# Second MLP product from fp16 halves, its halves made on GpSimd, norms of the input and the output partly moved to ScalarE and GpSimd

## The chip, the cores and the metric

One NeuronCore of one Trainium2 chip runs the whole program. The engines are TensorE (PE, its weight loads are PEld), VectorE (DVE), ScalarE (ACT), GpSimd (POOL) and the queue of SyncE (SP) that issues every DMA. The metric is the time of one execution in microseconds on the device. A profile of one execution, in which every instruction has a start and a duration, stands beside the times.

## What is computed

The reference, cut to what matters here (`LN` is a layer norm without gain):

```python
x = x + LN(attn(LN(x)))                      # 4 x 2048 x 256, dense attention: first part of the program
h0 = LN(x)
for l in range(2):                           # second part, window by window of 128 rows
    h = shift_token(h0)                      # half of the columns from the row before
    q, k, v = split(h @ wqkv[l])             # 3 x 512 columns, 8 heads of 64
    q, k = rotary(l2norm(q) * qs), rotary(l2norm(k) * ksc)
    o = local_attention(q, k, v)             # a window of 128 sees itself and the one before
    h0 = h0 + o @ wo[l]
    h = LN(shift_token(h0)) * lg + lb
    a, g = split(h @ w1[l] + b1[l])          # 2 x 682 columns
    h0 = h0 + (a * gelu(g)) @ w2[l] + b2[l]  # the second MLP product
x = x + LN(h0)
```

All in float32. The kernel keeps that precision by splitting an operand into a high and a low half and adding three products (high x high, high x low, low x high).

## The kernel before, in words

Rows are handled in windows of 128 rows: 64 windows in each of two layers, so 128 window steps (`NT`). The program has three stages: `phase_a` (dense attention, to 650 us), the preparation of the weights at the head of `phase_b` (650 to 717 us), and the main loop (717 us to the end), which is a software pipeline written out by hand. Each engine runs the same list of slots `s`; `run(s, r, pairs, layer)` holds, engine by engine, the code of one slot, and `slots` (L483) calls it with `r = s % 4`. In slot `s` window `s` has its q, k and v products, window `s-1` its scores, window `s-2` its probabilities times v and its output projection, window `s-3` the normalisation of its MLP input. The MLP itself goes in pairs of windows: in an **even slot** TensorE ends with the first MLP product (L944), in an **odd slot** with the second (L955). Both take inputs from VectorE, which multiplies a and gelu(g) into `hid` at the end of an even slot (L1174).

Nothing is scheduled automatically. The order on an engine is the order in which `run` is written, and an instruction that waits holds everything behind it on its engine or queue; the waits are semaphores. The order on TensorE in a slot: transposes of q and k of the window before (L847, L854), q, k, v products (L869), transposes of the probabilities (L885), probabilities times v (L897), scores (L910), output projection (L923), transpose of the next input (L836), then one of the two MLP products.

Lines that the prediction uses:

- ScalarE: squares of q and k (L981, L983), copies of the transposed probabilities to SBUF, four for a slot (L992), the cast of the attention's output (L995), the exponentials (L1002), gelu (L1015).
- VectorE: rotary terms (L1041 to L1043), statistics of the MLP input (L1107, L1109, L1111), its normalisation (L1117) and high half (L1120), the masked maximum of the scores (L1138), division by the row sum (L1151), `xp` (L1162, the stream after the attention), `xpp` (L1063, the stream after the MLP).
- GpSimd: the power -1/2 of the variance (L1200), the sum of squares by six halvings (L1190), the low half of the MLP input (L1205), sums of the rotary terms (L1209 for q, L1212 for k), the power of 16 sums of squares (L1223), k times its norm (L1228), `xb` (L1234).
- SyncE's queue, in the order of a slot: loads of the next input and tables, the DMA transpose of the halves of the MLP input of window `s-3` (L813), the store of `xp` of window `s-2` (L819), and its shifted load back as `h2` (L823, L824). The transpose waits for both halves:

```python
sp.wait: xh_hi, xh_lo of t = s-3  ->  dma_start_transpose(h2T, xh_hl)      # L813
sp.wait: xp_ready of t = s-2      ->  dma_start(xp_v, xp) -> load h2       # L819, L823, L824
```

## Time and profile before

| | value |
|---|---|
| median of 3 runs (lowest, highest) | 3122.34 us (3121.93, 3125.83) |
| the profiled execution | 3122.74 us, its span 3120.9 us |
| TensorE's granted clock, mean | 0.979 of full speed |
| PE busy | 2969.0 us, 95% |
| PEld busy | 2577.5 us, 83% |
| DVE busy | 2654.2 us, 85% |
| ACT busy | 1876.3 us, 60% |
| POOL busy | 1742.8 us, 56% |

The shares are means over the three stages and say little by themselves; the main loop is 77% of the span. A pair of slots (one even, one odd) takes 36.55 us in it, and 64 pairs make it up. "Busy" of TensorE counts overlapping matmuls once, and the time that one matmul adds is the distance between starts, not its duration.

### The profile page before, as it was taken

Reading aid. Unit: us, or ns where it says so; the run is one execution under the profiler, and the core shown is the slowest. Engines: PE = TensorE matmul, PEld = TensorE weight load, DVE = VectorE, ACT = ScalarE, POOL = GpSimd, SP = SyncE. Lnnn points to the kernel's source line nnn. Section 1 sums busy time; section 2 is a strip of 40 time slices with the busy share of each in tenths; the row PEclk is TensorE's granted clock in tenths of the full one; section 3 lists DMA queues with packets and bytes.
Section 4 is the critical chain, followed back from the end, with each engine's and each line's share of the span. In section 5 each row is a group of like instructions: output and inputs, shape, how many; then the busy total and the mean of one; then the engine's idle time right before and its main releaser. Section 6 shows DMA issues by size and latency. Waiting matters only on the chain.

```text
span 3120.9 us, 79791 instructions
## 1 busy us (share of the span) xinstructions
PE 2969.0 (95%) x24952; PEld 2577.5 (83%) x24952; DVE 2654.2 (85%) x7701; ACT 1876.3 (60%) x4322; POOL 1742.8 (56%) x2070
## 2 busy tenths in 40 slices
PE   7999999945999999999999999999999999999997
PEld 4868686844888888888888888888888888888886
DVE  7889898656888888888888888898999999999995
ACT  6252525113666666667666766666666667666763
POOL 0313131125666666666666666676776677767763
PEclk9999999967999999999999999999999999999998
DMA  1212121151111111111111111122221211122121
GB/s 39 62 48 64 46 63 40 54 202 53 47 50 49 56 47 50 52 49 47 50 54 50 49 54 48 51 57 61 61 56 58 59 55 55 58 64 59 56 58 43
DMA packets 273326, 177.65 MB, mean 57 GB/s; under 512 B 95758, under 2 KB 271090, under 8 KB 272754
## 3 DMA queue, kind: packets, MB, share of 16 engines
q1 hardware_dynamic: 273138, 175.50, 19.2%
q8 instruction: 74, 1.21, 0.2%
q14 instruction: 114, 0.93, 0.1%
HBM read 104.08 MB, written 54.54 MB: 51 GB/s over the span
## 4 chain that ended last, share of the span: by engine, by line
PE 73%; POOL 1%; issue 1%; DVE 1%; ACT 0%; DMA 0%; POOLq 0%; SPq 0%; DVEq 0%; ACTq 0%
PE b_ps L869 17%; PE b_ps L944 14%; PE b_ps L955 10%; PE b_ps L897 8%; PE b_ps L885 7%; PE b_ps L923 6%; PE b_ps L910 6%; PE b_ps L854 2%; PE b_ps L847 2%; PE b_ps L836 1%; POOL b_sq L1190 0%; POOL b_rn L1223 0%; DVE b_probs L1138 0%; POOL b_t L1212 0%; DVE b_probs L1151 0%
## 5 line engine op out<-in xcount | busy, mean ns | idle before, releaser
L1002 ACT ACTIVATE b_probs<-b_probs,b_negmax 128x256 f32<-128x256 f32 x1024 | 505.9, 495 | 78.4 <-DVE b_negmax L1138 77.5
L869 PE MATMUL b_ps<-b_wqkv,b_hT_hi 128*128 128x512 f32 x1536 | 492.0, 402 | 1.0 <-DVE b_hT_lo L1026 1.0
L944 PE MATMUL b_ps<-b_h2T,b_w 128*128 128x256 f16 x4224 | 474.4, 274 | 6.4 <-DMA b_h2T<-b_xh_hl 6.4
L944 PEld LDWEIGHTS b_ps<-b_h2T,b_w 128*128 128x128 f16 x4224 | 414.5, 98 | 55.3 <-DMA b_h2T<-b_xh_hl 6.8
L1190 POOL TENSOR_TENSOR b_sq<-b_sq 128x512 f32<-128x512 f32 (+5 forms) x768 | 418.5, 545 | 60.6 <-ACT b_sq L983 20.3
L1223 POOL TENSOR_TENSOR b_rn<-b_ss_min,b_mhalf 128x16 f32<-128x16 f32 x128 | 377.5, 2949 | 109.2 <-DVE b_ss_min L1050 109.0
L1151 DVE TENSOR_SCALAR b_probs<-b_probs,b_rinv 128x256 f32<-128x256 f32 x1024 | 409.6, 442 | 18.2
L1200 POOL TENSOR_TENSOR b_rstd<-b_var,b_mhalf 128x1 f32<-128x1 f32 x128 | 72.0, 562 | 552.9 <-DVE b_var L1111 552.9
L452 PE MATMUL a_ps<-a_xn_hl,a_E 128*128 128x256 f16 x3072 | 344.5, 273 | 8.8 <-DVE a_E L318 8.8
L955 PE MATMUL b_ps<-b_w,b_hid 128*128 128x256 f32 x1536 | 342.2, 379 | 1.2 <-DVE b_hid L1174 1.2
L452 PEld LDWEIGHTS a_ps<-a_xn_hl,a_E 128*128 128x128 f16 x3072 | 299.4, 98 | 44.2 <-ACT a_e L397 9.6
L869 PEld LDWEIGHTS b_ps<-b_wqkv,b_hT_hi 128*128 128x128 f32 x1536 | 282.7, 191 | 54.3 <-ACT b_hT_hi L967 1.4
L1138 DVE CUSTOM_DVE_ANT_0 b_probs<-b_ps,b_mask,b_rn 128x256 f32<-128x256 f32 x768 | 324.5, 478 | 0.0
L955 PEld LDWEIGHTS b_ps<-b_w,b_hid 128*128 128x128 f32 x1536 | 286.8, 190 | 37.9 <-DVE b_hid L1174 1.5
L869 PE MATMUL b_ps<-b_wqkv,b_hT_lo 128*128 128x512 f32 x768 | 302.7, 394 | 0.0
L992 ACT COPY b_probsT<-b_ps 128x512 f32<-128x512 f32 x512 | 264.0, 611 | 4.5 <-PE b_ps L885 4.2
L1015 ACT ACTIVATE b_gl<-b_ps,b_b,b_w_unit 128x256 f32<-128x256 f32 (+1 forms) x384 | 202.8, 561 | 102.8 <-DVE b_hid L1174 70.4
L897 PE MATMUL b_ps<-b_probsT,b_v 128*64 128x128 f32 x4096 | 252.3, 276 | 0.0
L885 PE MATMUL b_ps<-b_ident_f,b_probs 128*128 128x128 f32 x2048 | 245.5, 273 | 3.5 <-DVE b_xpp L1063 2.3
L885 PEld LDWEIGHTS b_ps<-b_ident_f,b_probs 128*128 128x128 f32 x2048 | 232.2, 141 | 20.0 <-DVE b_xpp L1063 2.5
L897 PEld LDWEIGHTS b_ps<-b_probsT,b_v 128*64 128x64 f32 x4096 | 221.4, 137 | 21.6 <-ACT b_probsT L992 18.1
L1174 DVE SCALAR_TENSOR_TENSOR b_hid<-b_ps,b_b1a,b_gl 128x256 f32<-128x256 f32 (+1 forms) x384 | 177.0, 478 | 53.3 <-ACT b_gl L1015 46.9
(139 smaller groups left out, 6218.8 us busy)
## 6 DMA issues: line engine op xcount, KB each, us to landing
b_hx<-xs_dram SPq DMA_DIRECT2D x256, 64.0 KB, 1.9
b_rot<-rot_dram SPq DMA_DIRECT2D x128, 128.0 KB, 2.1
b_xr<-xs_dram SPq DMA_DIRECT2D x128, 128.0 KB, 2.0
xp_dram<-b_xp SPq DMA_DIRECT2D x128, 128.0 KB, 1.8
b_h<-xp_dram SPq DMA_DIRECT2D x256, 64.0 KB, 1.8
a_x_res<-in_L_attn_x_dram SPq DMA_DIRECT2D x64, 128.0 KB, 2.2
x_dram<-a_x SPq DMA_DIRECT2D x64, 128.0 KB, 1.7
xs_dram<-a_xo SPq DMA_DIRECT2D x64, 128.0 KB, 1.8
```

Of the source, the lines that this page charges most:

```text
L452: last = nc.tensor.matmul(ps[:, bank, 0:D], E[:, j, a, i * P:(i + 1) * P], xn_hl[:, b % 2, j, c, :], start=(j == 0 and a == 0 and c == 0), ...
L869: last = nc.tensor.matmul(ps[:, bank, :], hT[:, k, :], wqkv[:, ds(layer(s), 1), part, k, bank * INNER:(bank + 1) * INNER], start=(k == 0 a ...
L885: last = nc.tensor.transpose(ps[:, 3 + p, n * P:(n + 1) * P], probs[:, 2 * p + n // 2, (n % 2) * P:(n % 2 + 1) * P], ident_f[:])
L897: last = nc.tensor.matmul(ps[h * DH:(h + 1) * DH, 7, p * P:(p + 1) * P], v[:, window, (2 * p + h) * DH:(2 * p + h + 1) * DH], probsT[:, p, ...
L944: last = nc.tensor.matmul(ps[:, bank, half * 2 * P:(half + 1) * 2 * P], w1[:, ds(layer(2 * j), 1), wp, k, first:first + P], h2T[:, hp, k, ...
L955: last = nc.tensor.matmul(ps[:, 3, n * D:(n + 1) * D], hid[:, c, n * P:(n + 1) * P], w2[:, ds(layer(2 * j), 1), c, :], start=(c == 0), sto ...
L992: nc.scalar.copy(probsT[:, p, :], ps[:, 3 + p, :]).then_inc(pT_kept, 1)
L1002: nc.scalar.activation(probs[:, h, :], probs[:, h, :], ACT.Exp, bias=negmax[:, h:h + 1], scale=-1.0, accum_out=rowsum[:, h:h + 1]).then_in ...
L1138: nc.vector.tensor_tensor_reduce(probs[:, h, :], head_scores(h), which, rn[:, (r - 1) % 2, h:h + 1], ABOVE_ALL, ALU.add, ALU.min, negmax[: ...
L1151: nc.vector.tensor_scalar(probs[:, h, :], probs[:, h, :], rinv[:, h:h + 1], None, ALU.mult).then_inc(probs_ready, 1)
L1190: nc.gpsimd.tensor_tensor(target, target, sq[:, :, width:2 * width], ALU.add).then_inc(ss_halved, 1)
L1223: nc.gpsimd.tensor_tensor(rn[:, r % 2, :], ss_min[:], mhalf[:], ALU.pow).then_inc(rn_ready, 1)
```

## The change

1. **Second MLP product.** `hid` and `w2` are split into fp16 halves, and the 12 float32 matmuls of a pair of windows become 36 fp16 ones. `w2` is scaled and split while the weights are prepared, which also takes new bounds (maxima of `w2` and the bias, a second reduction over partitions). The halves of `hid` are made by GpSimd: a cast and a subtraction for each of six blocks, four blocks at the end of the even slot, two in the odd slot.
2. **MLP input.** Statistics (`norm_stats`) stand ahead of `xpp` on VectorE; the addition of epsilon and a new term `shift2` go to GpSimd; the normalisation and the high half go to ScalarE as two ACTIVATE Identity, in the even slot ahead of the four copies of the probabilities, in the odd slot behind the cast of the attention's output. The low half (GpSimd) stays early in the even slot; in the odd slot it now stands behind `hid`'s halves and behind k's norm.
3. **Norms of q and k.** One halving on GpSimd and one VectorE reduction in place of six halvings; the power is taken in two parts of 8 columns, k's first.
4. **Output of layer 2.** Statistics and their power in the even slot, the normalisation itself on ScalarE in the odd slot.
5. **VectorE.** Two rotary instructions where three were, two reciprocals where four were, `xp` ahead of the divisions.
6. **ScalarE.** The copy of v stands behind the copies of the probabilities.

The diff, cut (semaphore names, allocations and renamed counts are left out):

```diff
@@ preparation of the weights
+                for l in range(LAYERS):
+                    nc.scalar.activation(w2[:, l, 0], w2_f[:, l], ACT.Copy, scale=w2_scale[:, l:l + 1]).then_inc(w2_hi, 1)
...
-                        pool.wait_ge(top_ready, LAYERS)
+                        pool.wait_ge(top_ready, 4 * LAYERS)
+                        nc.gpsimd.partition_all_reduce(top_all..., top..., P, RED_MAX).then_inc(top_shared, 1)
+                        nc.gpsimd.partition_all_reduce(sq_all[:], top_sq[:], P, RED_ADD).then_inc(top_shared, 1)
...
+                    nc.vector.scalar_tensor_tensor(w2[:, l, 1], w2_f[:, l], w2_scale[:, l:l + 1], w2[:, l, 0], ALU.mult, ALU.subtract)
@@ TensorE, odd slot
-                        pe.wait_ge(hid_ready, HC * (j + 1))
+                        pe.wait_ge(hid_lo, HC * (j + 1))
                         for n in range(2):
                             for c in range(HC):
-                                last = nc.tensor.matmul(ps[:, 3, n * D:(n + 1) * D], hid[:, c, n * P:(n + 1) * P], w2[:, ds(layer(2 * j), 1), c, :],
-                                                        start=(c == 0), stop=(c == HC - 1))
+                                for a, (hp, wp) in enumerate(PARTS):
+                                    last = nc.tensor.matmul(ps[:, 3, n * D:(n + 1) * D], hid_hl[:, hp, c, n * P:(n + 1) * P],
+                                                            w2[:, ds(layer(2 * j), 1), wp, c, :], ...)
@@ ScalarE
+                def normalise_input(t, r):
+                    if in_range(t):
+                        act.wait_ge(shift2_ready, t + 1)
+                        wait(act, xh_lo, t)
+                        nc.scalar.activation(xh[:], h2[:, (r - 3) % 2, :], ACT.Identity, bias=shift2[:], scale=rstd2[:]).then_inc(xh_ready, 1)
+                        wait(act, h2T_loaded, 16 * t)
+                        nc.scalar.activation(xh_hl[:, 0, :], h2[:, (r - 3) % 2, :], ACT.Identity, bias=shift2[:], scale=rstd2[:]).then_inc(xh_hi, 1)
...
                         nc.scalar.activation(sq[:, HEADS:2 * HEADS, :], by_head(ps[:, 1, :]), ACT.Square).then_inc(k_sq, 1)
+                    if r % 2 == 0:
+                        normalise_input(s - 3, r)
...
+                            nc.scalar.copy(probsT[:, p, :], ps[:, 3 + p, :]).then_inc(pT_kept, 1)
...
                         nc.scalar.copy(oT[:, 0], by_pair(ps[:, 7, :])).then_inc(oT_hi, 1)
+                    if r % 2 == 1:
+                        normalise_input(s - 3, r)
@@ VectorE
+                    norm_stats(s, r)
                     layer_output(pairs - 3, r, layer)
-                    (statistics of the MLP input)
                     rotate(s, r, 0, q_sq, q_terms, qr_ready)
-                        nc.vector.tensor_scalar(xh[:], h2[:, (r - 3) % 2, :], mv2[:, 0:1], rstd2[:], ALU.subtract, ALU.mult).then_inc(xh_ready, 1)
-                        nc.vector.tensor_copy(xh_hl[:, 0, :], xh[:]).then_inc(xh_hi, 1)
                     rotate(s, r, 1, k_sq, k_terms, kr_ready)
                     output_stats(pairs - 3, r, layer)
+                    sum_squares(s)
@@ GpSimd
+                        nc.gpsimd.tensor_scalar(var2[:], mv2[:, 1:2], EPS, None, ALU.add).then_inc(var2_ready, 1)
                         nc.gpsimd.tensor_tensor(rstd2[:], var2[:], mhalf[:, 0:1], ALU.pow).then_inc(rstd2_ready, 1)
+                        nc.gpsimd.tensor_scalar(shift2[:], mv2[:, 0:1], rstd2[:], -1.0, ALU.mult, ALU.mult).then_inc(shift2_ready, 1)
+                    if r % 2 == 1:
+                        hid_halves(pairs - 2, HID_EARLY, HC)     # cast and subtraction, blocks 4 and 5
+                    if r % 2 == 0:
+                        input_low(s - 3)
...
+                    if r % 2 == 1:
+                        input_low(s - 3)                         # behind kr
...
+                    if r % 2 == 0:
+                        hid_halves(pairs - 2, 0, HID_EARLY)      # blocks 0 to 3
```

The order on GpSimd in an odd slot of the main loop, in the kernel before, from the power of the variance to `xb`:

```order
L1200 TENSOR_TENSOR b_rstd2<-b_var2,b_mhalf 128x1 [waits b_var2_ready]
L1190 TENSOR_TENSOR b_sq<-b_sq 128x16x32 [waits b_ss_halved]
L1190 TENSOR_TENSOR b_sq<-b_sq 128x16x16 [waits b_ss_halved]
L1205 TENSOR_TENSOR b_xh_hl<-b_xh,b_xh_hl 128x256 [waits b_h2T_loaded]
L1209 TENSOR_TENSOR b_qr<-b_t1,b_t2 128x512 [waits b_qT_done,b_q_terms]
L1190 TENSOR_TENSOR b_sq<-b_sq 128x16x8 [waits b_ss_halved]
...
L1212 TENSOR_TENSOR b_t1<-b_t1,b_t2 128x512 [waits b_k_terms]
L1223 TENSOR_TENSOR b_rn<-b_ss_min,b_mhalf 128x16 [waits b_scores_kept]
L1228 TENSOR_TENSOR b_kr<-b_t1,b_rn 128x512 [waits b_kT_done,b_kr_sum,b_rn_ready]
L1234 TENSOR_TENSOR b_xb<-b_xp,b_b2 128x256 [waits b_xpp_ready]
```

The same place in the changed kernel (`b_hid_hl` are the halves of `hid`, `b_xh_hl` those of the MLP input, `b_rn_k` is k's norm):

```order
L1265 TENSOR_SCALAR b_var2<-b_mv2 128x1 [waits b_mv2_ready]
L1268 TENSOR_TENSOR b_rstd2<-b_var2,b_mhalf 128x1 [waits b_xh_hi,b_var2_ready]
L1270 TENSOR_SCALAR b_shift2<-b_mv2,b_rstd2 128x1 [waits b_rstd2_ready]
L1274 TENSOR_TENSOR b_sq<-b_sq 128x16x32 [waits b_k_sq]
L1246 CAST b_hid_hl<-b_hid 128x256 [waits b_hid_ready]
L1248 TENSOR_TENSOR b_hid_hl<-b_hid,b_hid_hl 128x256 [waits b_hid_hi]
...
L1282 TENSOR_TENSOR b_qr<-b_t1,b_t2 128x512 [waits b_qT_done,b_q_terms]
L1284 TENSOR_TENSOR b_t1<-b_t1,b_t2 128x512 [waits b_k_terms]
L1288 TENSOR_SCALAR b_ss_min<-b_ss 128x16 [waits b_ss_summed]
L1290 TENSOR_TENSOR b_rn_k<-b_ss_min,b_mhalf 128x8 [waits b_ss_ready]
L1294 TENSOR_TENSOR b_kr<-b_t1,b_rn_k 128x512 [waits b_kT_done,b_kr_sum,b_rnk_ready]
L1255 TENSOR_TENSOR b_xh_hl<-b_xh,b_xh_hl 128x256 [waits b_h2T_loaded]
```

The low half of the MLP input was the fourth instruction of the slot and is now behind k's product, with the two blocks of `hid` ahead of it as well.

The order on ScalarE in an even slot of the kernel before, from the cast of k to the cast of the attention's output:

```order
L977 CAST b_kT<-b_ps 128x4x128 [waits b_kT_done]
L981 ACTIVATE b_sq<-b_ps 128x512 [waits b_q_done,b_ss_ready]
L983 ACTIVATE b_sq<-b_ps 128x512 [waits b_k_done]
L986 COPY b_v<-b_ps 128x512 [waits b_pv_done,b_v_done]
...
L992 COPY b_probsT<-b_ps 128x512 [waits b_pT_done]
...
L995 CAST b_oT<-b_ps 128x512 [waits b_wo_done,b_pv_done]
```

And in the changed kernel:

```order
L1046 CAST b_kT<-b_ps 128x4x128 [waits b_kT_done]
L1051 ACTIVATE b_sq<-b_ps 128x512 [waits b_q_done,b_ss_summed]
L1055 ACTIVATE b_sq<-b_ps 128x512 [waits b_k_done]
L1034 ACTIVATE b_xh<-b_h2,b_shift2,b_rstd2 128x256 [waits b_xh_lo,b_shift2_ready]
...
L1036 ACTIVATE b_xh_hl<-b_h2,b_shift2,b_rstd2 128x256 [waits b_h2T_loaded]
...
L1063 COPY b_probsT<-b_ps 128x512 [waits b_pT_done]
...
L1067 COPY b_v<-b_ps 128x512 [waits b_pv_done,b_v_done]
L1072 CAST b_oT<-b_ps 128x512 [waits b_wo_done,b_pv_done]
```

Two instructions that wait for `shift2` now stand ahead of the four copies of the probabilities, and v's copy has moved behind them.

## Rows read from the trace of the kernel before

**Rows 1.** Busy time by stretch: stretch, length, then each engine, granted clock, DMA share.
```profile
900.00:1900.00 1000.00, 1000.00 (x8599) 892.51 (x8598) 863.77 (x2679) 686.75 (x1695) 641.00 (x728) 1.00 0.18 51
```

**Rows 2.** Timeline of PE, an odd and an even slot: start, duration, instruction.
```profile
1503.95 0.60 PE L847 MATMUL b_ps<-b_ident_f,b_qr 128*128 128x128 f32 x4
...
1516.05 5.34 PE L955 MATMUL b_ps<-b_w,b_hid 128*128 128x256 f32 x24
1521.23 0.60 PE L847 MATMUL b_ps<-b_ident_f,b_qr 128*128 128x128 f32 x4
...
1528.05 1.97 PE L897 MATMUL b_ps<-b_probsT,b_v 128*64 128x128 f32 x32
...
1533.30 7.37 PE L944 MATMUL b_ps<-b_h2T,b_w 128*128 128x256 f16 x66
1540.50 0.60 PE L847 MATMUL b_ps<-b_ident_f,b_qr 128*128 128x128 f32 x4
```

**Rows 3.** Groups of POOL by form: count, busy us, mean ns, idle before.
```profile
L1223 POOL TENSOR_TENSOR b_rn<-b_ss_min,b_mhalf 128x16 f32<-128x16 f32 x128 | 377.5, 2949 | 109.2 <-DVE b_ss_min L1050 109.0
L1212 POOL TENSOR_TENSOR b_t<-b_t 128x512 f32<-128x512 f32 x128 | 165.5, 1293 | 0.0
L1228 POOL TENSOR_TENSOR b_kr<-b_t,b_rn 128x512 f32<-128x512 f32 x128 | 133.4, 1042 | 10.0
L1205 POOL TENSOR_TENSOR b_xh_hl<-b_xh,b_xh_hl 128x256 f16<-128x256 f32 x128 | 86.4, 675 | 40.0 <-DVE b_xh_hl L1120 40.0
L1200 POOL TENSOR_TENSOR b_rstd<-b_var,b_mhalf 128x1 f32<-128x1 f32 x128 | 72.0, 562 | 552.9 <-DVE b_var L1111 552.9
L1190 POOL TENSOR_TENSOR b_sq<-b_sq 128x16 f32<-128x16 f32 x128 | 28.3, 221 | 10.0
L1196 POOL COPY b_mask_now<-b_mask 128x256 bf16 x27 | 11.6, 429 | 0.0
```

**Rows 4.** Timeline of ACT: the odd slot's squares of k, the even slot's copies.
```profile
1507.79 0.60 ACT L983 ACTIVATE b_sq<-b_ps 128x512 f32<-128x512 f32 x1 [0.72 <-PE b_ps L869]
...
1526.96 2.06 ACT L992 COPY b_probsT<-b_ps 128x512 f32<-128x512 f32 x4
```

**Rows 5.** Timeline of SyncE's queue, the odd slot's transpose, store and last load.
```profile
1512.10 1.22 SPq L813 DMA_TRANSPOSE b_h2T<-b_xh_hl  x1
1519.25 0.36 SPq L819 DMA_DIRECT2D xp_dram<-b_xp  x1
...
1521.65 0.38 SPq L824 DMA_DIRECT2D b_h<-xp_dram  x1
```

**Rows 6.** Timeline early in the loop, from a store of xp to the statistics.
```profile
787.79 0.35 SPq L819 DMA_DIRECT2D xp_dram<-b_xp  x1
...
791.82 0.42 DVE L1107 BATCH_NORM_STATS2 b_st<-b_h 128x6 f32<-128x256 f32 x1
792.38 0.18 DVE L1109 BATCH_NORM_AGGREGATE b_mv<-b_st 128x2 f32<-128x6 f32 x1
```

**Rows 7.** Groups of ACT by form: the exponentials and gelu.
```profile
L1002 ACT ACTIVATE b_probs<-b_probs,b_negmax 128x256 f32<-128x256 f32 x1024 | 505.9, 495 | 78.4 <-DVE b_negmax L1138 77.5
L1015 ACT ACTIVATE b_gl<-b_ps,b_b,b_w_unit 128x256 f32<-128x256 f32 x320 | 166.8, 561 | 101.0 <-DVE b_hid L1174 70.4 <-PE b_ps L944 28.9
```

**Rows 8.** Waits from 900 to 3100 us: total, times, longest.
```profile
PEld b_ps L897 <- ACT b_probsT L992: 17.7, 106, 0.2
```

**Rows 9.** Timeline of the preparation of the weights: low halves of w1.
```profile
697.56 9.15 POOL L613 TENSOR_TENSOR p_rot_all<-p_rot_all,p_head_scale 128x4096 f32<-128x4096 f32 x1 [6.92 <-issue]
697.96 11.71 DVE L672 SCALAR_TENSOR_TENSOR b_w<-p_w_f,p_w_scale,b_w 128x2816 f16<-128x2816 f32 x1
...
710.73 3.14 DVE L672 SCALAR_TENSOR_TENSOR b_w<-p_w_f,p_w_scale,b_w 128x2816 f16<-128x2816 f32 x1
```

**Rows 10.** Timeline of PE in the second slot of the loop.
```profile
737.11 1.12 PE L854 MATMUL b_ps<-b_ident_f,b_kr 128*128 128x128 f32 x4 [5.72 <-POOL b_kr L1228]
```

**Rows 11.** Group of DVE by form: the maximum over a layer's w1.
```profile
L654 DVE TENSOR_REDUCE p_top<-p_w_f 128x1 f32<-128x2816 f32 x2 | 6.2, 3086 | 0.1
```

More of the change, by code:

```diff
@@ new lines, in _ @@
+                    dve.wait_ge(top_ready, l + 1)
+                    nc.vector.tensor_tensor(top_sq[:, l:l + 1], top[:, 0, l:l + 1], top[:, 0, l:l + 1], ALU.mult)
+                dve.wait_ge(loaded_mlp, 16 * DMAS_MLP)
+                dve.wait_ge(cleared, 4)
+                for l in range(LAYERS):
+                    nc.vector.tensor_tensor(b1[:, l, :], ps[:, l, 0:W1_BLOCKS], b1_f[:, l, :], ALU.add).then_inc(bias_added, 1)
+                    nc.vector.tensor_reduce(top[:, 2, l:l + 1], w2_f[:, l].rearrange("p c d -> p (c d)"), AX.X, ALU.max, apply_absolute_value=True).then_inc(top_ready, 1)
@@ new lines, in _ @@
+                for l in range(LAYERS):
+                    dve.wait_ge(bias_added, l + 1)
+                    nc.vector.tensor_reduce(top[:, 1, l:l + 1], b1[:, l, :], AX.X, ALU.max, apply_absolute_value=True).then_inc(top_ready, 1)
+                    nc.vector.tensor_scalar(top_sq[:, l:l + 1], top_sq[:, l:l + 1], 2.0, None, ALU.mult).then_inc(top_ready, 1)
+                dve.wait_ge(top_shared, 2)
+                nc.vector.tensor_tensor(bias_sq[:], top_all[:, 1, :], top_all[:, 1, :], ALU.mult).then_inc(step, 1)
@@ L1166, in run @@
                     normalise(3)
-                    output_norm(pairs - 3, r, layer)
                     j = pairs - 2
                     if r % 2 == 0 and in_range(2 * j):
-                        wait(dve, w2_done, j)
+                        wait(dve, hid_lo, HC * j)
                         for c, bank in enumerate(W1_BANKS):
@@ L1234, in run @@
                         nc.gpsimd.tensor_tensor(xb[:, (r - 2) % 4, :], xp[:, r % 2, :], b2[:, ds(layer(t), 1), :], ALU.add).then_inc(xb_ready, 1)
+                    j = pairs - 3
+                    f = j - NW // 2
+                    if r % 2 == 0 and in_range(2 * j) and layer(2 * j) == 1:
+                        wait_apart(pool, mvf_ready, 2 * f + 2, passed_pool)
+                        nc.gpsimd.tensor_scalar(varf[:], mvf[:, :, 1], EPS, None, ALU.add).then_inc(varf_ready, 1)
+                        pool.wait_ge(varf_ready, f + 1)
+                        wait(pool, xf_ready, 2 * f)
+                        nc.gpsimd.tensor_tensor(rstdf[:], varf[:], mhalf[:, 0:2], ALU.pow).then_inc(rstdf_ready, 1)
+                        wait_apart(pool, rstdf_ready, f + 1, passed_pool)
+                        for n in range(2):
+                            last = nc.gpsimd.tensor_scalar(shiftf[:, n:n + 1], mvf[:, n, 0:1], rstdf[:, n:n + 1], -1.0, ALU.mult, ALU.mult)
+                        last.then_inc(shiftf_ready, 1)
+                    if r % 2 == 0:
+                        hid_halves(pairs - 2, 0, HID_EARLY)
                     j = pairs - 3
```

288 lines of the change are left out of this document (159 added, 129 removed).

## The prediction

> **What bounds the kernel now.** I read the busy times by stretch first. In a stretch of 1000 us in the main loop TensorE is busy for all of it, at full clock, VectorE for 864 us and GpSimd for 641 us [rows 1]. The loop is bound by TensorE, so work taken from it is gained unless another chain takes over. Then TensorE's timeline, to get the length of each slot and the distances: the odd slot goes from 1503.95 to 1521.23 (17.28 us), the even one to 1540.50 (19.27 us), 36.55 us a pair; the second product takes 1521.23 - 1516.05 = 5.18 us of the odd one, the first product 1540.50 - 1533.30 = 7.20 us for 66 fp16 matmuls [rows 2]. Then the other engines' timelines, to see how much later each thing that TensorE waits for may come. The closest is in the list of waits: the weight loads of "probabilities times v" (L897) waited for ScalarE's copy 106 times, 0.17 us each [rows 8], so that copy arrives with little to spare in nearly every slot.
>
> **The second product.** 66 matmuls in 7.20 us is 0.109 us for one of fp16 with 256 columns. 36 of them are 3.93 us, where 24 halves of float32 matmuls took 5.18 [rows 2]. TensorE is relieved of 1.25 us a pair, 80 us over 64 pairs, and the odd slot becomes 16.03 us.
>
> **What the moved steps do to the queue.** I follow one pair, with 0 at the start of its odd slot. The squares of k end at 1507.79 + 0.60, which is 4.44 [rows 4]; the power of the variance is over at about the same time. GpSimd then has, in order: one halving of 512 columns; cast and subtraction of two blocks of `hid`; the sums for q and k; a floor of 16 columns; a power of 8; k times its norm; and only then the low half of the MLP input. The sums are 1.29 each, the halving the same size (1.29), subtraction and low half 0.67, k's product 1.04, the floor 0.22 [rows 3]. The power took 0.56 for 1 column and 2.95 for 16, 0.159 a column, so 1.68 for 8 [rows 3]. The cast isn't in the trace: from below a bf16 copy of 256 columns, 0.43, less what a float32 source might save (nothing that I can show, so I allow 0.2), from above the subtraction's 0.67, as it reads less [rows 3]; I take 0.43, the nearest row. With 0.07 for each of four waits on a result just made: 4.5 + 1.29 + 2 x (0.43 + 0.07 + 0.67) + 2 x 1.29 + 0.22 + 0.07 + 1.68 + 0.07 + 1.04 + 0.67 = 14.4. Before, the transpose that waits for it went out 7.15 us ahead of the store of `xp` [rows 5], so its place cost nothing.
>
> Now it does. SyncE's queue waits for this low half before the transpose, and behind the transpose stand the store of `xp` and its load back. Transpose 0.3 after the low half, 1.22 of issue, 0.2 to the next: the store goes out at 16.15, though `xp` is made earlier than before, when the store went at 1519.25, which is 15.30 [rows 2, 5]. From a store's issue to the statistics of the loaded rows it was 791.82 - 787.79 = 4.03 us where VectorE was waiting for them [rows 6]; in the main loop the last load is issued 2.40 after the store [rows 5], 0.2 more. So `h2` is there at 20.35, which is 4.3 after the start of the even slot (at 16.03).
>
> **What then waits.** In the even slot VectorE, which is past the low halves of q and k at about 2.6, waits for `h2` until 4.3. From statistics to mean and variance 0.74 [rows 6]: 5.1. On GpSimd: epsilon 0.2, power 0.56, shift 0.2 [rows 3], and 0.35 of waits: 6.4. ScalarE has no such ACTIVATE in its rows; by exponentials (0.50) and gelu (0.56) with 0.1 overlap, two of 256 columns take 0.9 to 1.0, from below 0.8 (two exponentials, each 0.1 overlapped), from above 1.1 (two of gelu's) [rows 7]. The first copy of the probabilities starts at 7.4. It started at 1526.96, which is 5.73 after the slot's start [rows 2, 4]. How late may it start? It lasts 0.6, and probabilities times v starts at 6.82 [rows 2], with 0.17 of slack already used by waiting weight loads [rows 8]; later copies follow at 0.49 and the products at 0.47, so nothing is caught up. I take 6.05 as the limit. TensorE then stands for 7.4 - 6.05 = 1.35 us in every even slot, and I add 0.15 for GpSimd being held once by VectorE's divisions, which fall into the same stretch: 1.5 us. Against the 1.25 us saved, a pair becomes 0.25 us longer.
>
> That last 0.15 rests on a pair of rows: the same VectorE instruction took 11.71 us beside a GpSimd multiplication of 9.15, and 3.14 without it [rows 9]. The Trainium skill ("SBUF — State Buffer", Who interferes with whom) has this as an exclusive lock of a port that the two engines share, held for a whole instruction by whoever starts first. By that rule, the trace agrees (9.15 + 3.14 is 12.3, less the part where they did not overlap), and one more collision would be worth 0.3 us at most.
>
> The Trainium skill ("GPSIMD Engine Reference", 3.1 Elementwise) puts one-input work at about 1.03 cycles an element and two-input work at 2.6. By the first the cast would be about 0.22 us plus its start, an estimate from that page, and the sum would fall by 0.1 to 0.2 us a pair; no row here has a float32 cast on GpSimd, so the sum goes by the rows above.
>
> **The other edits.** VectorE loses the normalisation and the high half, two of four reciprocals and some rotary overhead and gains one reduction; it was not the bound [rows 1], and its gain is idle time. ScalarE's two ACTIVATE in the odd slot stand ahead of the exponentials and push them by 0.9; the low half of the next input then comes within 0.1 of its need in the even slot, and up to 0.7 late if a GpSimd addition is in the way. That stall would lie in front of the same wait for the copies and so be a part of the 1.5, not on top of it. `hid`'s halves are ready by 8.0 of the odd slot, TensorE wants them at 12.1: nothing. The first product's input in the even slot still has some 2 us to spare. The output's norm moves to where ScalarE idles between the squares; GpSimd has at most 1.5 us more of it per pair, behind which stand `hid`'s first four blocks, and those have room: nothing.
>
> **Outside the steady loop.** Preparation: VectorE's chain runs from the maxima (3.09 for 2816 columns, so 1.7 for the 1536 of `w2`, twice [rows 11]) through some fifteen tiny steps instead of five (+2), then the low halves of `w2` (3.14 x 1536/2816, 1.7 twice [rows 9]) and its share of a wait on the second reduction (+1). 3.4 + 2 + 3.4 + 1 and 0.7 for small pieces: 10.5 us, from 4 (if part of it lies under loads) to 16. Filling of the pipeline: TensorE waited 5.72 us for k's norm [rows 10], and the slot behind it about as long; in this chain one halving replaces six (-2.0), a power of 8 one of 16 (-1.3), so 3.1 less twice, and `xp` ahead of the divisions gives about 1.2 twice: -8.5, from -12 to -4. End: the last halves of `hid` stand alone (+1.1, cast and subtraction), and two more hand-overs: +2.5, less or more by 2.
>
> **Sum.** The stall falls in 61 pairs. 3122.74 (the profiled execution: its span of 3120.9 and 1.8 around it) - 80 + 61 x 1.5 + 10.5 - 8.5 + 2.5 = 3138.7. The profiled execution is 0.4 above the median of the runs shown, so I forecast 3138 us.
>
> **Range of this case.** The chain is long, and each 0.1 us in it is 6 us of time. With the low ends (cast 0.23, no waits, two ACTIVATE at 0.8, the copy's limit 0.3 later) the stall is near 0.5: 3078. With the high ends (cast 0.67, power of 8 at 2.0, waits 0.15, two collisions) near 2.4: 3193.
>
> **Rivals.**
>
> *A: the chain has slack, TensorE stays the bound.* The low half of the MLP input comes soon enough, or the store isn't held by it. For it: the chain crosses two slots, and `xp` itself is made earlier, ahead of four divisions. Against it: the queue is in order, and the start of the copies leaves 0.3 us. With no stall: 3122.74 - 80 + 4.5 = 3047. With a stall of 0.5 it passes into the low end above. It decides once the stall is under 1.24 us (61 x 1.24 is the 80 saved less the 4.5 added outside the loop). This is the faster side.
>
> *B: GpSimd becomes the bound.* Per pair it had 23.4 us of work (0.641 of 36.55 [rows 1]). Out go 4.0 of halvings, in come 6.6 for the halves of `hid`, 0.6 to 1.2 for the powers and 1.2 for small ones: 28 to 29 us, in layer 2 some 31.5, of the 35.3 a pair would have. Against it: there remain 4 us, and what it waits for is early. For it: ten instructions more per pair than before, most in chains of two, and waits between them that a sum of durations doesn't hold. At 0.4 us more for each it would be full, and with its fixed places late everywhere: a stall of some 3 us a pair, 3122.74 - 80 + 61 x 3 + 4.5 = 3230. This is the rule of the other side too: the Trainium skill ("GPSIMD Engine Reference", 4.1 Engine selection) would keep elementwise work of two inputs on VectorE, being about twice slower on GpSimd.
>
> *C: nothing to be seen.* Stall and saving cancel within 0.1 us a pair, a point inside the forecast's range: 3117 to 3128.
>
> **Chances.** Forecast with a stall from 1.0 to 2.4: 0.55. A (under 1.0): 0.33, of which no stall at all 0.13. B: 0.12. C lies in the forecast's case with 0.12. 0.2% is 6.2 us, about what a measurement of this kernel can tell from no change. Faster 0.35, the same 0.12, slower 0.53. The range leaves out the clean gain and most of B: 3065 to 3190.
>
> **What would show it.** TensorE's odd slots 16.0 us long in the timeline, with the second product at 3.9; even slots 20.8 instead of 19.3, with TensorE idle ahead of probabilities times v, released by ScalarE's copies. ScalarE waiting for `shift2` in even slots, VectorE's statistics waiting there for the load of `h2` until 4.3 after the slot's start, SyncE's queue waiting for GpSimd's low half in odd slots and storing `xp` about 2.4 us after it is made. The low half at 14.4. The loop begins 10 us later. I am wrong if statistics in even slots wait for nothing, if the low half is done before 13 in the odd slot, or if TensorE waits somewhere else, for k or for `hid`.

## The result and the profile after

The changed kernel took 3188.1 us (median of 4 runs, 3183.9 to 3190.1), the kernel before 3122.1 us beside it: a ratio of 1.0207, 95% interval 1.019 to 1.0225. Slower was forecast, and 3188 lies within the range, but only 16 us of loss were forecast and 66 came.

The busy times of the stretch that [rows 1] shows of before:

```profile
900.00:1900.00 1000.00, 964.07 (x8697) 840.34 (x8696) 772.28 (x2255) 726.37 (x1769) 740.64 (x970) 1.00 0.17 49
```

TensorE, busy for all of the stretch before, now stands for 36 us of it at the same full clock. GpSimd rose from 641 to 741 us, which is 27.8 of the 37.48 us of a pair, far from full: rival B is out. The timeline of PE, an odd slot and the even slot behind it, against [rows 2]:

```profile
1526.42 0.60 PE L898 MATMUL b_ps<-b_ident_f,b_qr 128*128 128x128 f32 x4
...
1538.57 4.09 PE L1007 MATMUL b_ps<-b_w,b_hid_hl 128*128 128x256 f16 x36
1542.50 0.60 PE L898 MATMUL b_ps<-b_ident_f,b_qr 128*128 128x128 f32 x4
...
1544.54 0.73 PE L920 MATMUL b_ps<-b_wqkv,b_hT_hi 128*128 128x512 f32 x2 [1.00 <-DVE b_hT_lo L1105]
...
1549.15 1.96 PE L936 MATMUL b_ps<-b_ident_f,b_probs 128*128 128x128 f32 x16
1551.30 2.11 PE L948 MATMUL b_ps<-b_probsT,b_v 128*64 128x128 f32 x32 [0.19 <-ACT b_probsT L1063]
...
1556.69 7.37 PE L995 MATMUL b_ps<-b_h2T,b_w 128*128 128x256 f16 x66
1563.90 0.49 PE L898 MATMUL b_ps<-b_ident_f,b_qr 128*128 128x128 f32 x3
```

The odd slot is 16.08 us long (17.28 before), the even one 21.40 (19.27): the whole gain of the fp16 product, 1.20 us, is there, and 2.13 us are lost behind it. The pair is 37.48 instead of 36.55. Probabilities times v (L948) starts 8.80 us after the slot's start, 6.82 before. The idle time in front of it carries three names in the list of waits from 900 to 3000 us (total, times, longest):

```profile
DVE b_st L1133 <- DMA b_h<-xp_dram: 66.1, 56, 3.3
PE b_ps L920 <- DVE b_hT_lo L1105: 41.3, 52, 1.0
PEld b_ps L948 <- ACT b_probsT L1063: 27.4, 104, 0.4
PE b_ps L936 <- DVE b_xpp L1149: 24.9, 43, 2.1
```

The first row is the forecast wait of VectorE for the load of `h2`. The third is the copies. The second and fourth, for the low half of the next QKV input and for `xpp`, were not in the sum. The idle times are smaller than the stall, because a stop also ends the overlap of two matmuls: q, k and v start 1.25 us later in their slot than before (2.04 us after its start against 0.79), and the row shows 1.00 of it as idle.

The forecast chain, in the same two slots: GpSimd and SyncE's queue at the end of the odd slot, then VectorE, GpSimd and ScalarE in the even one (against [rows 4, 5]).

```profile
1540.41 0.67 POOL L1255 TENSOR_TENSOR b_xh_hl<-b_xh,b_xh_hl 128x256 f16<-128x256 f32 x1
1541.40 1.22 SPq L864 DMA_TRANSPOSE b_h2T<-b_xh_hl  x1
1542.74 0.50 SPq L870 DMA_DIRECT2D xp_dram<-b_xp  x1
...
1545.27 0.38 SPq L875 DMA_DIRECT2D b_h<-xp_dram  x1
...
1547.26 0.43 DVE L1133 BATCH_NORM_STATS2 b_st<-b_h 128x6 f32<-128x256 f32 x1 [1.24 <-DMA b_h<-xp_dram]
...
1548.14 0.88 DVE L1149 SCALAR_TENSOR_TENSOR b_xpp<-b_ps,b_w_unit,b_xb 128x256 f32<-128x256 f32 x2
...
1549.31 0.26 POOL L1270 TENSOR_SCALAR b_shift<-b_mv,b_rstd 128x1 f32<-128x1 f32 x1 [0.21 <-POOL b_rstd L1268]
...
1549.68 0.60 ACT L1034 ACTIVATE b_xh<-b_h,b_shift,b_rstd 128x256 f32<-128x256 f32 x1 [1.45 <-POOL b_shift L1270]
1550.19 0.59 ACT L1036 ACTIVATE b_xh_hl<-b_h,b_shift,b_rstd 128x256 f16<-128x256 f32 x1
1550.68 2.02 ACT L1063 COPY b_probsT<-b_ps 128x512 f32<-128x512 f32 x4
```

Read it against the slot's start at 1542.50: store at 0.24, statistics at 4.76, shift done at 7.07, first copy at 8.18. `xpp` stands behind the statistics on VectorE, so the same load holds it too.

The distance from one first MLP product to the next, taken over the loop, says how much of the 67.4 us of span (3188.3 - 3120.9) lies where. Before, the median was 36.56 us; after, 37.47, and a few pairs at the loop's start, at the turn of the layers and at the end took 38.2 to 39.4. From the first such product (806.31, before 802.08) to the last (3162.60, before 3096.41) the loop lost 62.0 us; 4.2 were lost ahead of it and 1.2 behind.

### The profile page after: what moved, and what is told of

It reads as the page before. It is cut to its first block and busy times, and to the rows that moved or that the text cites. A ratio compares the mean times of both kernels' runs of the same rounds, so it can differ in the third digit from the quotient of the medians.

```text
span 3188.3 us, 81609 instructions
## 1 busy us (share of the span) xinstructions
PE 2936.1 (92%) x25720; PEld 2504.8 (79%) x25720; DVE 2481.0 (78%) x6734; ACT 2039.5 (64%) x4644; POOL 2063.0 (65%) x2807
## 5 line engine op out<-in xcount | busy, mean ns | idle before, releaser
L920 PE MATMUL b_ps<-b_wqkv,b_hT_hi 128*128 128x512 f32 x1536 | 500.9, 408 | 52.2 <-DVE b_hT_lo L1105 43.7
L1197 DVE CUSTOM_DVE_ANT_0 b_probs<-b_ps,b_mask,b_rn 128x256 f32<-128x256 f32 x768 | 317.6, 478 | 0.0
L1166 DVE TENSOR_TENSOR b_oT<-b_ps,b_oT 128x512 fp32r<-128x512 f32 x128 | 88.5, 691 | 279.0 <-ACT b_oT L1072 279.0
L1248 POOL TENSOR_TENSOR b_hid_hl<-b_hid,b_hid_hl 128x256 f16<-128x256 f32 (+1 forms) x384 | 258.2, 672 | 31.0
L948 PE MATMUL b_ps<-b_probsT,b_v 128*64 128x128 f32 x4096 | 260.3, 280 | 9.9 <-ACT b_probsT L1063 5.9
L1007 PE MATMUL b_ps<-b_w,b_hid_hl 128*128 128x256 f16 x2304 | 261.9, 273 | 3.0 <-POOL b_hid_hl L1248 3.0
L948 PEld LDWEIGHTS b_ps<-b_probsT,b_v 128*64 128x64 f32 x4096 | 217.6, 137 | 47.5 <-ACT b_probsT L1063 28.5
L1007 PEld LDWEIGHTS b_ps<-b_w,b_hid_hl 128*128 128x128 f16 x2304 | 224.7, 98 | 29.0 <-POOL b_hid_hl L1248 3.2
L1265 POOL TENSOR_SCALAR b_var<-b_mv 128x1 f32<-128x1 f32 x128 | 29.8, 233 | 312.2 <-DVE b_mv L1136 312.2
```

Of the source, the lines that this page charges most:

```text
L920: last = nc.tensor.matmul(ps[:, bank, :], hT[:, k, :], wqkv[:, ds(layer(s), 1), part, k, bank * INNER:(bank + 1) * INNER], start=(k == 0 a ...
L948: last = nc.tensor.matmul(ps[h * DH:(h + 1) * DH, 7, p * P:(p + 1) * P], v[:, window, (2 * p + h) * DH:(2 * p + h + 1) * DH], probsT[:, p, ...
L1007: last = nc.tensor.matmul(ps[:, 3, n * D:(n + 1) * D], hid_hl[:, hp, c, n * P:(n + 1) * P], w2[:, ds(layer(2 * j), 1), wp, c, :], start=(c ...
L1197: nc.vector.tensor_tensor_reduce(probs[:, h, :], head_scores(h), which, rn[:, (r - 1) % 2, h:h + 1], ABOVE_ALL, ALU.add, ALU.min, negmax[: ...
L1248: nc.gpsimd.tensor_tensor(hid_hl[rows, 1, c, :], hid[rows, c, :], hid_hl[rows, 0, c, :], ALU.subtract).then_inc(hid_lo, 1)
```

## The experiments

Each ratio is against the kernel before, run beside it on the same chip; its medians there were 3121.9 to 3124.1 us. "Pair" is the median distance from one first MLP product to the next, in layer 1 and layer 2. The first row is the kernel before as it ran beside the changed one.

| kernel | us | ratio (95%) | pair 1, 2 |
|---|---|---|---|
| before | 3122.1 | 1 | 36.56, 36.56 |
| changed | 3188.1 | 1.0207 (1.019-1.0225) | 37.47, 37.46 |
| e1_act_behind | 3240.6 | 1.037 (1.0353-1.0388) | 38.03, 38.46 |
| e2_xpp_first | 3193.1 | 1.0222 (1.0205-1.0239) | 37.43, 37.41 |
| e3_both | 3127.2 | 1.0011 (1.0002-1.0021) | 36.28, 36.52 |
| e4_two_products | 3194.3 | 1.0225 (1.0208-1.0242) | 37.50, 37.49 |
| b1_low_late | 3301.4 | 1.0574 (1.0557-1.0592) | 39.10, 39.72 |
| e5_low_earlier | 3124.5 | 1.0006 (0.9997-1.0016) | 36.46, 36.47 |
| e6_low_keep | 3109.5 | 0.9955 (0.9938-0.9971) | 35.83, 36.74 |
| e7_keep_only | 3188.2 | 1.0209 (1.0192-1.0226) | 37.44, 37.47 |
| e8_all | 3077.2 | 0.9856 (0.984-0.9873) | 35.75, 35.67 |
| e9_store_first | 3131.6 | 1.0029 (1.0018-1.0041) | 36.56, 36.45 |
| e10_low_keep_xpp | 3155.1 | 1.0102 (1.0085-1.0119) | 36.57, 37.50 |
| e11_all_store | 3091.7 | 0.9903 (0.9887-0.992) | 35.77, 36.13 |

**Is it TensorE's work at all? (e4)** One of the three products that make the second MLP product is left out (high halves by low halves), a third of its matmuls.

```diff
-for a, (hp, wp) in enumerate(PARTS):
+for a, (hp, wp) in ((0, (0, 0)), (2, (0, 1))):
```

> Changed kernel with a third of the second MLP product left out (the product of hid's low half and w2's high half, 12 of 36 matmuls); the rest unchanged. It leaves out part of the computation. TensorE is relieved of 12 x 0.109 = 1.31 us in each odd slot, at its end. Theory (a chain that begins at k's squares in the odd slot and runs over GpSimd, SyncE's queue, the store and load of xp, statistics and normalisation to probabilities times v in the next even slot sets the pair): the work stands beside this chain, the even slot's stall grows by what the odd slot loses, 3188 us, within 6. Rival (TensorE is the bound and a fixed stall is added to it): 3188 - 64 x 1.31 = 3104 us.

It took 3194.3 us, 6 above the changed kernel and at the edge of what was expected (the granted clock was a little lower too, 0.971 against 0.978): taking out a third of these matmuls gained nothing. The timeline of PE shows an odd slot shorter by 1.31 us and an even slot longer by 1.18:

```profile
1528.23 0.60 PE L898 MATMUL b_ps<-b_ident_f,b_qr 128*128 128x128 f32 x4
...
1543.00 0.60 PE L898 MATMUL b_ps<-b_ident_f,b_qr 128*128 128x128 f32 x4
...
1565.58 0.60 PE L898 MATMUL b_ps<-b_ident_f,b_qr 128*128 128x128 f32 x4
```

14.77 and 22.58 us, against 16.08 and 21.40 (the median even slot of layer 1 is 22.74). With the stall, what TensorE saves in the odd slot it waits out in the even one: its time is no longer the pair's time.

**Which link holds TensorE? (e2, e1, e3)** e2 puts `xpp` ahead of the output's statistics on VectorE, e1 puts ScalarE's even normalisation behind the copies of the probabilities, e3 does both.

```diff
-norm_stats(s, r)
 layer_output(pairs - 3, r, layer)
+norm_stats(s, r)
```
```diff
-if r % 2 == 0:
-    normalise_input(s - 3, r)
 (copies of the probabilities, L1063)
+if r % 2 == 0:
+    normalise_input(s - 3, r)
```

> Changed kernel, but on VectorE xpp (L1149) stands ahead of the statistics of the MLP input, as it did before the change. Theory (two chains): the transposes of the probabilities start 0.9 us earlier in even slots, but the copies still stand behind the normalisation, so that probabilities times v starts as late: 3188 us, within 5. Rival (xpp behind the late statistics is the cause): 1.2 us a pair gone, 3115 us.

> Changed kernel, but in even slots ScalarE's two normalising ACTIVATE stand behind the four copies of the probabilities, ahead of v's copy. Theory (two chains from the late load of h2 end at TensorE nearly together: one by the normalisation on ScalarE to the copies, one by xpp on VectorE, since the transposes of the probabilities in even slots wait for xpp): only the first is cut, the second still holds the transposes until 6.8 after the slot's start; TensorE's even slot shortens by the 0.2 to 0.3 us between the two, 3188 - 61 x 0.25 = 3173 us. Rival (the normalisation ahead of the copies is the cause, as predicted): the whole stall beyond what k's and q's products wait for goes, 1.2 us a pair, 3115 us.

> Changed kernel with both edits: xpp ahead of the statistics, and the normalisation behind the copies in even slots. Theory (two chains): h2 still lands as late (4.8 after the even slot's start), but nothing that TensorE needs soon hangs on it; left is the stall in front of the q, k, v products, 0.85 us in even slots, for which the low half of the next input comes late (the odd slot's normalisation pushes the exponentials). Even slot 20.1 us, pair 36.2: 3188 - 61 x 1.3 = 3109 us. Rival (the stall is a matter of GpSimd being full, so that it moves elsewhere): 3170 to 3190 us.

e2 held, 5 us above the changed kernel: the wait for `xpp` vanished from the list of waits, and the copies' waits grew by more (in the changed kernel 27.4 us for PEld and 4.4 us in 17 times for PE):

```profile
PEld b_ps L948 <- ACT b_probsT L1063: 59.8, 104, 1.3
PE b_ps L948 <- ACT b_probsT L1063: 41.4, 56, 1.1
```

e1 missed both theories: 3240.6, where a gain had been expected. Its rows, PE, SyncE's queue, VectorE and GpSimd in the even slot that starts at 1517.42, and last two groups of VectorE's divisions later in that slot:

```profile
1518.39 0.51 SPq L870 DMA_DIRECT2D xp_dram<-b_xp  x1
...
1522.84 0.43 DVE L1133 BATCH_NORM_STATS2 b_st<-b_h 128x6 f32<-128x256 f32 x1 [2.24 <-DMA b_h<-xp_dram]
...
1524.72 1.96 PE L936 MATMUL b_ps<-b_ident_f,b_probs 128*128 128x128 f32 x16 [1.49 <-DVE b_xpp L1149]
...
1528.67 0.68 POOL L1255 TENSOR_TENSOR b_xh_hl<-b_xh,b_xh_hl 128x256 f16<-128x256 f32 x1 [2.27 <-ACT b_xh_hl L1036]
...
1533.82 1.93 DVE L1209 TENSOR_SCALAR b_probs<-b_probs,b_rinv 128x256 f32<-128x256 f32 x4
...
1536.74 1.09 DVE L1209 TENSOR_SCALAR b_probs<-b_probs,b_rinv 128x256 f32<-128x256 f32 x2
```

TensorE no longer waits for the copies but for `xpp`, and the chain has become longer: the store goes out 0.97 us after the slot's start (0.24 in the changed kernel), because GpSimd, held 2.27 us by the later normalisation, is late for the rest of the even slot. The way from there to the store leads over VectorE. A division takes 0.35 us alone. In the changed kernel only GpSimd's `xb` (0.7 us) falls beside the divisions, and one of them takes 0.82; in e1 k's product (1.04 us, from 1534.04) falls beside one of the first four, which takes 1.14, and `xb` (from 1536.69) beside one of the last two, which takes 0.82. The eight of an even slot take 4.03 us instead of 3.26 (medians of layer 1), so the statistics of the next odd slot start 3.18 us into it instead of 2.61, GpSimd waits for them, and the low half, the transpose and the store move with them. That the overlap lengthens the divisions is read from these rows; no run takes it away alone. So each of the two moves alone opens one of two doors behind the same load. With both open (e3) the time fell by 61 us, to 3127.2, 18 above what I expected: q, k and v still wait 24.2 us in all for `hT_lo`, and layer 2 is 0.24 us a pair longer than layer 1. In e3 the load of `h2` is even later than in the changed kernel (statistics 5.43 us into the even slot against 4.77, medians of layer 1); TensorE just doesn't wait for it.

**Is it the late low half? (b1, e5, e9)** b1 makes this one move in the kernel before. e5 moves it back by a power and a product in the changed kernel. e9 leaves GpSimd alone and lets the store pass the transpose on the queue.

```diff
 (b1, in the kernel before; e5 the reverse, to behind kr_sum)
-input_low(s - 3)            # behind halve(s, 0, 2)
+if r % 2 == 1: input_low(s - 3)   # behind the product kr
```
```diff
 (e9, odd slots)
-transpose of xh_hl (s-3); store of xp, loads of h2 (s-2)
+store of xp, loads of h2 (s-2); transpose of xh_hl (s-3)
```

> One part of the change alone: in the kernel before, only the odd slots' second half of the MLP input is moved, from behind the first halvings to behind the key product (before 1511.10 in a slot that begins at 1503.95, then about 1520.2 on GpSimd). Theory (the chain odd GpSimd, transpose, store of the output, load of the next MLP input, statistics, ScalarE is what the move lengthens): the transpose is issued about 1521.1 and the store about 1522.5 against 1519.25 before, so the MLP input lands 3.2 us later in the even slot and the copies of the probabilities start about 3.4 us late; 2 to 3.4 us for each of 61 pairs, 3240 to 3330 us. Rival (the move falls into slack, and the loss of the changed kernel is GpSimd's new work or TensorE's): 3122 +- 6 us.

> The changed kernel with one instruction moved back: the odd slots' second half of the MLP input stands behind the key terms' sum, ahead of the power for the key product (about 11.5 us into the slot instead of 14.1). Theory (the same chain): the store then waits for the output alone, about 13.9 us into the slot against 16.3, so the MLP input lands 2.4 us earlier in the even slot, ScalarE's normalisation ends before TensorE's transposes of the probabilities, and both the wait for the copies (about 1.1 us) and that for the shortcut (0.5 us) go; the wait for the second half of the QKV input (0.85 us) stays. Pair of slots 36.6 to 36.9 us against 37.49: 3133 to 3151 us. Rival (the waits for copies and shortcut come from GpSimd's work on the odd slot as a whole, whatever its order): 3188 +- 6 us.

> The changed kernel with one move on the DMA queue: in odd slots the store of the attention output and the loads of the next MLP input stand ahead of the transpose of the MLP input's halves; GpSimd's order stays as changed, with its odd second half at 14.1 us. Theory (the late second half costs only because the transpose that waits for it stands ahead of the store in the queue): the store goes at about 13.9 us instead of 16.3, and the time is that of the kernel with the second half moved back, 3118 to 3132 us. Rival (the order on GpSimd itself, or the late transpose, costs): 3175 to 3200 us.

b1: +179 us by this move alone, 2.9 us a pair, inside the theory's 3240 to 3330. But the door was another than I had named. There VectorE itself normalises, and the wait for the load holds everything behind it on that engine, the attention's output `oT` at last (SyncE's queue, VectorE, TensorE):

```profile
1533.78 0.51 SPq L819 DMA_DIRECT2D xp_dram<-b_xp  x1
...
1538.36 0.43 DVE L1107 BATCH_NORM_STATS2 b_st<-b_h 128x6 f32<-128x256 f32 x1 [3.38 <-DMA b_h<-xp_dram]
...
1543.35 0.67 DVE L1090 TENSOR_TENSOR b_oT<-b_ps,b_oT 128x512 fp32r<-128x512 f32 x1
...
1544.08 2.63 PE L923 MATMUL b_ps<-b_wo,b_oT 128*128 128x256 f32 x12 [1.94 <-DVE b_oT L1090]
```

Not all of the 179 us is waiting. From 900 to 3100 us TensorE stood 110.4 us in 56 times for `oT`, and its granted clock fell to the lower level behind half of these stops (29 times, 99 us in all, each time within 1.5 us of the first matmul behind one), as in the stretch that begins with the last row (length, busy times, clock):

```profile
1544.00:1547.00 3.00, 2.92 (x15) 2.86 (x16) 3.00 (x15) 2.54 (x11) 2.66 (x6) 0.58 0.22 44
```

The 12 matmuls of that row took 2.63 us where they take 1.68 at full clock. Over the loop the clock was 0.98 (900 to 1900 us) and 0.97 (2000 to 3000 us), against 1.00 in both for the kernel before and the changed one. 99 us at half the clock do the work of 50, so up to some 50 of the 179 us, an estimate, are the price of the lower clock behind the waits and not the waits themselves.

e5: 3124.5 us, 64 less than the changed kernel (I had said 3133 to 3151; the pair is 36.46, a little under my 36.6). The same place, SyncE and PE:

```profile
1516.91 1.22 SPq L864 DMA_TRANSPOSE b_h2T<-b_xh_hl  x1
1518.90 0.36 SPq L870 DMA_DIRECT2D xp_dram<-b_xp  x1
...
1521.14 0.60 PE L898 MATMUL b_ps<-b_ident_f,b_qr 128*128 128x128 f32 x4
...
1522.95 0.72 PE L920 MATMUL b_ps<-b_wqkv,b_hT_hi 128*128 128x512 f32 x2 [0.78 <-DVE b_hT_lo L1105]
...
1527.24 1.91 PE L936 MATMUL b_ps<-b_ident_f,b_probs 128*128 128x128 f32 x16
1529.08 1.97 PE L948 MATMUL b_ps<-b_probsT,b_v 128*64 128x128 f32 x32
```

The store goes 2.24 us ahead of the even slot's start instead of 0.24 behind it, the waits for `xpp` are gone, those for the copies are back near their size of before (19.6 us of weight loads in 106 times, 17.7 before), and one is left, for `hT_lo`. e9 held at 3131.6. Its rows, SyncE's queue and GpSimd in the odd slot from 1510.83 to 1526.91:

```profile
1524.67 0.35 SPq L873 DMA_DIRECT2D xp_dram<-b_xp  x1
1524.82 0.67 POOL L1265 TENSOR_TENSOR b_xh_hl<-b_xh,b_xh_hl 128x256 f16<-128x256 f32 x1
...
1527.82 1.22 SPq L865 DMA_TRANSPOSE b_h2T<-b_xh_hl  x1
```

The low half starts 13.99 us into the slot, as late as in the changed kernel, but the store goes 2.24 us ahead of the even slot, as in e5, and 57 of the 66 us of loss are gone. So it is the order on the queue, the store behind a transpose that waits for GpSimd, that carries the delay; that is shown from both sides.

**The wait under the wait (e7, e6)** Both make `hT_lo` ahead of the second group of divisions on VectorE, e7 in the changed kernel, e6 in e5.

```diff
-normalise(2)
 if in_range(s + 1):
     keep_hT(s + 1)
+normalise(2)
```

> The changed kernel with one move on VectorE: the QKV input's second half is made ahead of the second group of probability products, so that q, k and v no longer wait for it in the even slots. Theory (the waits of an even slot lie over one another, and the one that ends last is ScalarE's normalisation ahead of the copies, at 8.8 us of the slot): what TensorE gains at q, k and v it loses at the shortcut and the copies; pair of slots 37.4 to 37.5 us as in the changed kernel, 3188 +- 8 us. Rival (the waits add up, each with a price of its own): 3120 to 3147 us, since this wait alone is 0.7 to 1.1 us in each of 61 pairs.

> As the kernel with the second half of the MLP input moved back (e5), and on VectorE the QKV input's second half made ahead of the second group of probability products instead of inside it. Theory: hT_lo is ready about 0.6 us into the even slot instead of 1.6, TensorE's q, k and v no longer wait, pair 35.8 to 36.0 us: 3080 to 3100 us, faster than the kernel before by 1%. Rival (the products made later then hold up the transposes or the next exponentials): no faster than e5.

e7 gave 3188.2, as the theory said. `hT_lo` is started at once (0.2 us into the slot that starts at 1504.71), and TensorE meets the next wait instead:

```profile
1504.91 0.42 DVE L1105 TENSOR_TENSOR b_hT_lo<-b_ps,b_hT_hi 128x256 fp32r<-128x256 f32 x1 [0.68 <-ACT b_hT_hi L1020]
...
1511.48 1.96 PE L936 MATMUL b_ps<-b_ident_f,b_probs 128*128 128x128 f32 x16 [1.45 <-DVE b_xpp L1149]
```

The same edit on top of e5, where the load is early, gives 15 us (e6, 3109.5). It missed its 3080 to 3100: layer 1 came to 35.83 as expected, but in layer 2, where GpSimd also has the last norm, `xpp` was late again, 20.0 us in 27 times:

```profile
2529.22 1.96 PE L936 MATMUL b_ps<-b_ident_f,b_probs 128*128 128x128 f32 x16 [0.75 <-DVE b_xpp L1149]
```

**All together (e8, e10, e11)** e8 has all four moves: e5's on GpSimd, e7's and e2's on VectorE, e1's on ScalarE. e10 leaves out e1's; e11 has e9's in place of e5's.

> All four moves together: as e6, and also the shortcut ahead of the output statistics on VectorE and ScalarE's even normalisation behind the copies of the probabilities. Theory: with the MLP input early, nothing is left for the last two moves to save, and the even normalisation behind the copies only delays GpSimd's even half; equal to e6 within 6 us or slower by up to 30. Rival (the copies are still held up by the normalisation): faster than e6 by over 10 us.

> Three of the four moves of the fastest kernel so far: the odd second half moved back, the QKV input's second half ahead of the products, the shortcut ahead of the output statistics; ScalarE's even normalisation stays ahead of the copies. Theory (of the kernel without the last two, the waits for the shortcut, 20.0 us in all, 27 times, are what the third move takes away; the rest up to the fastest belongs to the normalisation): 3085 to 3100 us. Rival (the normalisation ahead of the copies costs nothing with the input early): 3077 +- 5 us.

> As the kernel with all four moves, but with the store ahead of the transpose on the DMA queue in odd slots in place of GpSimd's second half moved back. Theory (the two are two ways to take the same wait out of the store's way): 3077 +- 8 us. Rival (the later transpose holds up the first MLP product of the even slot): 3090 to 3130 us.

e8 took 3077.2 us, 1.4% faster than the kernel before and 111 us faster than the changed one; the theory (no better than e6) fell, and the rival was right. TensorE is full again:

```profile
900.00:1900.00 1000.00, 998.60 (x9121) 883.10 (x9120) 844.03 (x2348) 757.31 (x1847) 781.89 (x1021) 1.00 0.18 51
```

e10 missed both theories: 3155.1, 46 slower than e6, by the move that should have saved 20. The timeline of ACT and PE in its even slot, which starts at 1523.96:

```profile
1530.38 0.60 ACT L1034 ACTIVATE b_xh<-b_h,b_shift,b_rstd 128x256 f32<-128x256 f32 x1 [1.87 <-POOL b_shift L1270]
...
1531.99 2.12 PE L948 MATMUL b_ps<-b_probsT,b_v 128*64 128x128 f32 x32 [0.97 <-ACT b_probsT L1063]
```

`xpp` ahead of the statistics delays them by its 0.8 us, and with ScalarE's normalisation still ahead of the copies that comes out in full on TensorE. Moves e1 and e2 are one move in two halves: a half alone never gained (in the changed kernel e1 cost 52 us and e2 5; on top of e6 e2's half cost 46, and e1's half was not tried there), both together gain.

e11 (3091.7) lies 7 us outside its theory and just inside the rival's range, but not for the rival's reason: the first MLP product follows the output projection as closely as in e8 (1.87 and 1.88 us from start to start, medians of layer 2). Layer 1 is e8's (35.77), layer 2 is 0.46 a pair longer, where TensorE waits for `qT_low` (15.1 us of weight loads in 26 times, 0.3 in e8). Why only there is open.

## Why the prediction was right in its course and wrong in its size

**Right.** The low half ended at 14.66 in the pair shown (forecast 14.4, low half of 0.67 included), the store was held by the transpose, `xp` had been made 2.5 us earlier, VectorE waited for `h2`, ScalarE for the shift, TensorE ahead of probabilities times v. The odd slot is 16.08 (16.03). The mechanism is shown by b1, e5 and e9. Rival A (TensorE the bound) and B (GpSimd full) fell by e4 and by the busy times; B also by e9, which leaves GpSimd's work and order as they were. The high end of the range was worked out as 3193 and given as 3190; the measured time is under both.

**The step that failed** is "What then waits": the stall was sized at 1.5 us a pair and measured 2.13. The mechanism was the forecast one; the terms of this sum were too small. Against the even slot's start they were (the last column is what each step adds to the error):

| | forecast | measured | adds |
|---|---|---|---|
| store issued | 0.12 | 0.24 | +0.12 |
| statistics start | 4.3 | 4.76 | +0.34 |
| shift done | 6.4 | 7.07 | +0.21 |
| first copy starts | 7.4 | 8.18 | +0.11 |
| latest start of the copy without a stall | 6.05 | 6.20 | -0.15 |
| delay of L948 | 1.35 | 1.98 | = +0.63 |
| longer L948 | 0 | 0.14 | +0.14 |
| GpSimd held once by VectorE | 0.15 | 0 | -0.15 |
| stall | 1.5 | 2.13 | = +0.63 |

The load was the worst: from the store's issue to the statistics 4.52 us (4.56 in the pair before), where I took 4.03 from [rows 6] and 0.2 for the later load. The store is now issued straight behind the transpose and takes 0.50 us of the queue instead of 0.36 [rows 5], and the last load follows it by 2.53 us instead of 2.40; that the rest is the transpose's traffic I did not test. On GpSimd epsilon and shift were 0.23 and 0.26 where I had 0.2 each, and the waits around the three came to 0.50 in this pair where I had 0.35. The normalisation starts 0.11 after the shift, a hand-over for which the sum had nothing. Two rows of GpSimd by form, for the power and the cast of the odd slot:

```profile
L1290 POOL TENSOR_TENSOR b_rn_k<-b_ss_min,b_mhalf 128x8 f32<-128x8 f32 x128 | 214.0, 1672 | 10.7
L1246 POOL CAST b_hid_hl<-b_hid 128x256 f16<-128x256 f32 x320 | 126.9, 397 | 100.3 <-DVE b_hid L1231 83.7 <-issue 16.6
```

The power of 8 (1.67, I had 1.68) and the cast (0.40, I had 0.43) were right. By the Trainium skill ("GPSIMD Engine Reference", 3.1 Elementwise) the cast would take 0.22 us plus its start, an estimate from that page's 1.03 cycles an element; the rows show 0.40, and no run here shows the start by itself.

The four errors up to the first copy have the same sign and make 0.78 us. Two things took 0.30 back, and that was luck: the copy could start 0.15 later than I allowed (L948 starts 0.62 us after it, little more than the copy's own 0.56, and I had kept 0.17 of slack), and the collision didn't happen, for from statistics to shift it is 2.05 us from start to start in even slots and 2.04 in odd ones (medians of layer 1). With the 0.14 of the longer L948 the rest is 2.13 - 1.5 = 0.63 us a pair. The loop was to lose 61 x 1.5 - 63 x 1.25 = 13 us over the 63 distances and lost 62; of the 49 missed, 61 x 0.63 = 38 are this; the odd slot's 0.05 is another 3, and what is left, some 7, fits the few long pairs at the seams, which I had not thought of.

**A wait missed, without price.** I didn't see that `xpp` stands behind the statistics, and put `hT_lo` at 0.1 late with 0.7 at most, where it was 1.00. Neither changed the time: e2 and e7 took these waits away and TensorE met the next one. That such a stall would be a part of the one at the copies I had written, and it held. They count once the load is early: the one for `hT_lo` from e5 to e6 (0.63 us a pair in layer 1), the one for `xpp` in e6's layer 2.

**Outside the loop** the terms were near enough. Preparation cost 9.7 (first work of the loop at 728.70, before 719.03; forecast 10.5), filling gave back 5.5 (8.5), the end cost 1.2 (2.5). The lock that [rows 9] showed came again, in rows of the preparation:

```profile
702.56 10.36 POOL L629 TENSOR_TENSOR p_rot_all<-p_rot_all,p_head_scale 128x4096 f32<-128x4096 f32 x1 [7.06 <-issue]
704.17 10.23 DVE L715 SCALAR_TENSOR_TENSOR b_w<-p_w_f,p_w1a_scale,b_w 128x1408 f16<-128x1408 f32 x1
714.32 1.67 DVE L715 SCALAR_TENSOR_TENSOR b_w<-p_w_f,p_w_scale,b_w 128x1408 f16<-128x1408 f32 x1
```

VectorE's first instruction here started 1.61 us after GpSimd's and took 10.23 us, where one of the same shape took 1.67 alone. The Trainium skill ("SBUF — State Buffer", Who interferes with whom) has a port that the two engines share, held for a whole instruction by whoever starts first, and the trace agrees.
